# Routing the tokens of a mixture of experts inside the attention stage, and running 25 full tiles while the last batches are routed

## What is computed

```
x = x + xattn(layernorm(x), ctx, ctx, gates..., outnorm_weight)     # per head: C = (q k^T / sqrt(32)) * D; C / normalizer; C v; head norm
x = x + ffn(layernorm(x), w12, w3, gate_w)

scores = einsum('btd,ed->bte', x, gate_w)
topk_scores, topk_idx = top_k(scores, 2);  topk_probs = softmax(topk_scores)
h1, h2 = split(einsum('btd,ehd->bteh', x, w12));  hidden = silu(h1) * h2       # H = 512
y = sum over the row's two experts of prob * einsum('bteh,edh->bted', hidden, w3)
```

## Time and profile before

| | |
|---|---|
| median of 3 runs | 655.87 us (653.12 to 657.32) |
| profiled execution | 654.9 us, of it 653.1 us between first and last instruction |
| TensorE matmul / weight load | 564.8 us (86%) / 466.0 us (71%) |
| VectorE | 451.9 us (69%) |
| ScalarE | 348.5 us (53%) |
| POOL | 296.5 us (45%) |
| mean granted TensorE clock | 0.933 of full speed |

### The profile page before, as it was taken

The page is one execution under the profiler, slowest core; times in us unless marked ns, Lnnn a source line. Parts: engine busy times, 40 slices in busy tenths (PEclk is TensorE's granted clock), DMA queues, the critical chain, the costliest instruction groups (busy, mean ns, idle before and its releaser), DMA issues.

```text
span 653.1 us, 14222 instructions
## 1 busy us (share of the span) xinstructions
PE 564.8 (86%) x3612; PEld 466.0 (71%) x3613; DVE 451.9 (69%) x987; ACT 348.5 (53%) x769; POOL 296.5 (45%) x312
## 2 busy tenths in 40 slices
PE   3779879999989951239999999999999999999993
PEld 1334668888878840127888888888888888888882
DVE  4664586787777778946667677667767767767762
ACT  2456556777777755014555555555555555555551
POOL 5423136365455534032555555555555555555532
PEclk9899998999999955559999999999999999999998
DMA  7875336787776668921433333333333333433322
GB/s 231 252 225 162 91 93 185 200 212 197 210 219 172 193 161 244 279 50 17 66 50 50 62 51 50 62 52 50 62 52 50 59 54 49 59 55 49 59 40 24
DMA packets 66018, 73.44 MB, mean 112 GB/s; under 512 B 12762, under 2 KB 55776, under 8 KB 65984
## 3 DMA queue, kind: packets, MB, share of 16 engines
q0 software_dynamic: 18240, 28.17, 25.1%
q1 hardware_dynamic: 38528, 36.21, 19.1%
q10 hardware_dynamic: 9216, 8.65, 3.9%
HBM read 43.51 MB, written 19.01 MB: 96 GB/s over the span
## 4 chain that ended last, share of the span: by engine, by line
issue 40%; POOL 15%; PE 14%; DVE 14%; DMA 10%; ACT 4%; SPq 1%; ACTq 0%; DVEq 0%; POOLq 0%
POOL xg L1168 9%; DMA out_rows<-ys,index 6%; PE bank L1287 5%; POOL out_rows L1177 4%; PE dots L1269 3%; DVE ohn L996 2%; DMA w12h<-in_x 2%; DVE ohp L995 2%; DVE c L846 1%; DVE st L727 1%; PE dots L1222 1%; ACT x2n L636 1%; PE bank L1336 1%; PE dots L1220 1%; DVE tot L887 1%
## 5 line engine op out<-in xcount | busy, mean ns | idle before, releaser
L1177 POOL DMA_INDIRECT out_rows<-ys,index x71 | 112.5, 1585 | 156.1 <-DVE ys L1048 145.1
L1054 DVE TENSOR_TENSOR w3l<-w,w3h 128x1024 fp32r<-128x1024 f32 x71 | 87.2, 1229 | 30.9 <-issue 29.7
L1168 POOL DMA_INDIRECT xg<-token_table,index x71 | 70.4, 992 | 46.1 <-DVE index L1013 24.4
L693 ACT CAST w3h<-w 128x1024 fp32r x71 | 74.4, 1048 | 20.4 <-issue 20.4
L1409 PE MATMUL bank<-w3l,hth 128*128 128x256 f32 x284 | 76.5, 302 | 1.8 <-DVE w3l L1054 1.8
L1410 PE MATMUL bank<-w3h,hth 128*128 128x256 f32 x284 | 70.8, 282 | 0.0
L1287 PE MATMUL bank<-aug,c 128*128 128x99 f32 (+2 forms) x512 | 63.9, 279 | 6.0 <-DVE c L846 5.9
L1287 PEld LDWEIGHTS bank<-aug,c 128*128 128x128 f32 x512 | 60.8, 195 | 11.0 <-DVE c L846 10.3
L1048 DVE TENSOR_SCALAR ys<-bank,pc 128x256 f32<-128x256 f32 x71 | 34.4, 484 | 46.6 <-PE bank L1413 46.6
L1031 DVE TENSOR_TENSOR htl<-bank,hth 128x512 fp32r<-128x512 f32 x71 | 49.1, 692 | 25.2 <-ACT hth L683 25.2
L1381 PE MATMUL weighs<-w12l,xh 128*128 x144 | 62.3, 432 | 1.1 <-DVE xl L1020 1.1
(11 more groups left out here) (172 smaller groups left out, 1235.1 us busy)
## 6 DMA issues: line engine op xcount, KB each, us to landing
w12l<-in_w12T SPq DMA_DIRECT2D x24, 256.0 KB, 3.5
aug<-in_ctxv SPq DMA_DIRECT2D x16, 264.0 KB, 3.5
w12h<-in_x SPq DMA_DIRECT2D x16, 256.0 KB, 3.6
w12l<-in_ctxT SPq DMA_DIRECT2D x16, 256.0 KB, 3.6
qbd<-w12h SPq DMA_DIRECT2D x64, 64.0 KB
x<-in_x SPq DMA_DIRECT2D x16, 256.0 KB, 3.3
out_rows<-x ACTq DMA_DIRECT2D x16, 256.0 KB, 2.5
token_table<-x2n ACTq DMA_DIRECT2D x16, 256.0 KB, 3.5
```

The lines of the kernel that those rows point to most:

```text
L693: nc.scalar.copy(W3H[i][:], w3[:, bass.ds(e, 1)].rearrange("p a k d -> p (a k d)")).then_inc(w3h_ready, 1)
L1054: v.tensor_tensor(W3L[i][:], w3[:, bass.ds(e, 1)].rearrange("p a k d -> p (a k d)"), W3H[i][:].bitcast(F32), ALU.subtract).then_inc(w3l_re ...
L1168: q.indirect_dma_start(out=XG[x][:], out_offset=None, in_=table, in_offset=bass.IndirectOffsetOnAxis(ap=index[:, j:j + 1], axis=0)).then_i ...
L1177: q.indirect_dma_start(out=out, out_offset=bass.IndirectOffsetOnAxis(ap=index[:, j:j + 1], axis=0), in_=YS[o][:], in_offset=None, compute_ ...
```

## The change

Four parts, in this order through the kernel.

- *Routing in groups*: batches are routed in five groups, `GROUPS` (0 to 2, 3 to 5, 6 and 7, 8 to 11, 12 to 15). A row's rank within its expert is carried on from group to group (`seen`), its place is 4096 times the expert plus the rank, and POOL scatters pairs of row number and probability to these places of a table in memory (`place`, 64 scatters of 128 pairs of 8 bytes). A list of tiles is fetched from the table (`fetch_list`), turned by TensorE and copied into `index`, `prob`, `etab` and `clear`.
- *Two phases of tiles*: the first 25 (`FIRST`) tiles are full ones of batches 0 to 7 and are listed in step 15. Steps 16 to 18 and the separate routing are gone: what was in them stands in `remains(j)` of each engine, between the instructions of tiles 0 to 21. The first 28 tiles are written out, the others looped (VectorE writes out all).
- *Weight pieces*: the eight late ones are handled in steps 4 to 7, two in each (`load_free`, `free_pieces`, `free_low`); the low parts of the last two of the sixteen are made by VectorE (`last_low`). `piece_high` handles batch b-1 in step b, not b-2.
- *Third weights*: SyncE fetches the 512 KB of a tile's expert two tiles ahead (`load_w3`); `w3` is gone. The row's probability comes from `prob`, so `pc` and its wait are gone.

The diff's core, in the order of the engines' blocks: SyncE, ScalarE (`free_pieces`, `remains`), VectorE (the loop over steps), POOL.

```diff
+CUT = B // 2
+FIRST = (CUT * S * TOPK - NE * (P - 1) + P - 1) // P
+GROUPS = ((0, 3), (3, 6), (6, CUT), (CUT, 12), (12, B))
...
+            def load_free(s):
+                if s == 0:
+                    sp.wait_ge(cols_ready, 2)
...
+                for n in (2 * s, 2 * s + 1):
+                    at = (W1 + n) * HID
+                    sp.dma_start(room(flat_l, W1 + n, HID), w12T[:, at:at + HID]).then_inc(free_in, 16)
...
+            def load_w3(j, i):
+                wait(sp, w3l_ready, j - 1)
+                e = sp.value_load(etab[0:1, bass.ds(j, 1)], min_val=0, max_val=NE - 1)
+                sp.dma_start(W3[i][:], w3T[:, bass.ds(e * (KH * E), KH * E)]).then_inc(w3_in[i], 16)
...
+            def free_pieces(s):
+                act.wait_ge(free_in, 32 * (s + 1))
+                for n in (2 * s, 2 * s + 1):
+                    at = slice((W1 + n) * HID, (W1 + n + 1) * HID)
+                    nc.scalar.copy(flat_h[:, at], room(flat_l, W1 + n, HID)).then_inc(free_hi, 1)
+                act.wait_ge(free_hi, 2 * s + 1)
+                wait(act, free_added, 16 * s)
+                nc.scalar.mul(minus2[:], room(flat_h, W1 + 2 * s, HID), -1.0).then_inc(free_minus, 1)
...
+            def remains(j):
+                if j == 1:
+                    turned(B - 3)
+                    squares(B - 1, SQ[:])
+                if j == 2:
+                    row_scales(B - 2)
+                    head_scales(B - 1)
+                if j == 3:
+                    normal_rows(B - 2)
+                    store_rows(B - 2)
+                if j == 4:
+                    turned(B - 2)
+                if j == 5:
+                    row_scales(B - 1)
+                if j == 6:
+                    normal_rows(B - 1)
+                    store_rows(B - 1)
+                if j == 7:
+                    turned(B - 1)
+                if j == 9:
+                    odds(len(GROUPS) - 1)
...
+            for b in range(B):
+                i = b % 2
+                if has(b, 1):
+                    far(b - 1)
+                combine(b, 0)
...
+                    if b == hi + 3:
+                        largest(gr, 1)
+                        chosen(gr)
+                if has(b, 1):
+                    centre(b - 1)
...
+                    if b == hi + 4:
+                        slots(gr, RANKS)
+                        chances(gr)
+                        if gr == 2:
+                            counts(0, RANKS[:, 64:64 + NE])
+                if b == GROUPS[2][1] + 5:
+                    list_rows(0)
+                if has(b, 2):
+                    row_statistics(b - 2)
+                combine(b, 1)
+                if b == B - 1:
+                    take_list(0, RANKS)
...
+                    if b == hi + 2:
+                        largest(gr, 0)
+                if FREE_AT <= b < FREE_AT + FREE_STEPS:
+                    free_low(b - FREE_AT)
...
+            def place(g, lo, hi):
+                k0 = group(g)[2]
+                pool.wait_ge(slots_ready, g + 1)
+                pool.wait_ge(pairs_ready, g + 1)
+                for k in range(k0 + lo, k0 + hi):
+                    q.indirect_dma_start(out=places, out_offset=bass.IndirectOffsetOnAxis(ap=slot[:, k:k + 1], axis=0),
+                                         in_=pairs[:, k, :], in_offset=None).then_inc(placed, 16)
...
+                if has(b + 1, 0):
+                    weighted(b + 1, 1 - b % 2)
...
+                if b in (8, 9, 10):
+                    place(0, 4 * (b - 8), 4 * (b - 7))
+                if b in (11, 12):
+                    place(1, 6 * (b - 11), 6 * (b - 10))
+                if b == 13:
+                    place(2, 0, 5)
+                if b == 14:
+                    place(2, 5, 8)
...
             for j in range(NX - 1):
                 gather(j)
+            mix(B - 2)
             for j in range(TILES + 1):
...
+                if j == 3:
+                    mix(B - 1)
                 if j >= 1:
                     add(j - 1)
+                if j in (1, 2):
+                    place(3, 2 * (j - 1), 2 * j)
+                if 4 <= j < 10:
+                    place(3, 2 * (j - 2), 2 * (j - 1))
+                if 11 <= j < 19:
+                    place(4, 2 * (j - 11), 2 * (j - 10))
+                if j == 19:
+                    fetch_list(1)
```

More of the change, by code:

```diff
@@ L305, in expert_tiles, with has @@
                 step(TILES // NX * NX + x, x)
+        def has(b, back):
+            return 0 <= b - back < B
         def stages(j):
@@ new lines, in odds @@
+            def odds(g):
+                nt = group(g)[1]
+                act.wait_ge(r_diff, g + 1)
+                nc.scalar.activation(ex[:, 0:nt], diff[:, 0:nt], ACT.Exp).then_inc(r_exp, 1)
+            weights(0, 0)
+            for b in range(B):
+                i = b % 2
+                if has(b, 1):
+                    near(b - 1)
+                state(b, i)
+                if has(b, 3):
+                    turned(b - 3)
+                weights(b, 1)
+                if b == 0:
@@ L1056, in _ @@
+            last_low(B - 2)
+            take_scores(B - 4, SCORES)
+            last_low(B - 1)
+            far(B - 1)
             low(0, 0)
-            dve.wait_ge(w3_in, 16 * NE)
-            dve.wait_ge(tables, 1)
-            expert_tiles(dve, expert)
+            for j in range(TILES + 1):
+                expert(j, j % 2)
         @block.gpsimd
@@ L1384, in half_up @@
                     ins.then_inc(up_ready, 1)
+                if isinstance(j, int) and j == FIRST:
+                    pe.wait_ge(tables, 2)
                 if up:
```

1076 lines of the change are left out of this document (594 added, 482 removed).

## The result

The changed kernel takes 706.88 us, the kernel before 656.16 (medians of 4 runs each): ratio 1.073, 95% interval 1.061 to 1.085. Slower, as forecast, but by 51 us where 16 were forecast.

The account below looks back on a forecast made before the run. Bounds: mutual engine waits in attention, 61.8 us with nearly no matmul, then TensorE in the tiles. Terms: 654.9 - 56.9 + 14.8 + 3.6 + 16 + 28 + 7.8 + 3 = 671.2 us; range 628 to 692.

Parts of the forecast that it names:

- The gap: Between last attention matmul and first tile matmul: listing the first 25 tiles early lets tiles start at 233.3, gaining 56.9 us.
- Eight weight pieces: Steps 4 to 7: VectorE's tot waits behind ScalarE's casts, 3.7 us a step, +14.8 us; routing in steps 6 and 7, +3.6.
- 32 scatters: POOL, steps 8 to 14: 1.3 us each, half counting in the two-step loop, VectorE's 10.6 us beside: +16 us (11 to 26).
- The list in step 15: Seam after attention: list ready at 227.7, with 0.3 us for POOL to start, inside the gap's gain.
- Batches 13 to 15 inside the tiles: Early tiles: table loads and waits for statistics, +28 us; clock falls behind waits at tiles 2, 5 and 9, +7.8 us.
- POOL in tiles 11 to 18: POOL work of 5.5 us against 4.87 in eight tiles, partly covered by two ys buffers, plus expert turns: +3 us.
- Third weights: Tiles: 512 KB fetched per tile within 6.7 us of room, so hidden, cost 0.
- 1: Rival: inserted work fits into idle time, 618 us, chance 0.20; in one of two stages only, 642 to 647, 0.10.
- 2: Rival, cheap ends: placings at 0.58 us and no fall of the clock, 658 us, no difference; chance 0.20.
- 3: Rival: a placing costs what an adding scatter does, POOL becomes the bound in the tiles, 690 us; chance 0.10.
- 4: Rival: a table load costs the 2.83 us that the rows leave open, 686 us; chance 0.05.
- 5: Rival: third weights late in every tile, 7.5 us from issue to landing, 728 us; chance 0.03.

Follow-up runs that it names:

- b1: Kernel before, with nine more unused VectorE instructions (128x48) in each of steps 4 to 13, behind the first c: 678.71 us, +22.7.
- e3: Changed kernel with 20 filler matmuls of 128 columns in each of steps 5 to 8, ahead of the key-value product: 697.14 us.
- c5: c3 with e7's swap and ten filler matmuls in each of steps 6 to 15: 678.01 us, 2.9 more than without the filler.
- b2: Kernel before, with four more scatters of 128 pairs of 8 bytes behind vw in each of steps 4 to 13: 695.26 us, +39.3.
- c2: Changed kernel, placings ahead of vw, free weight pieces later in mid-step, mix ahead of step 15's list, one function table in tiles 2 and 5: 678.07 us.
- e1: Changed kernel with POOL's placings in steps 8 to 14 ahead of vw instead of behind it: 689.35 us, 14.8 less.
- c3: c2 with SyncE loading aug and kn ahead of the rows x: 672.98 us.
- e7: Changed kernel with SyncE's fetch of third weights two tiles ahead placed before the order of additions: 708.44 us, 4.3 more.
- e6: Changed kernel with third weights fetched for the first two tiles only, 69 of 71 fetches left out: 698.96 us, 5.2 less.
- e5: Changed kernel with one function table for logarithm and exponential in tiles 2 and 5, 6 loads for 10: 702.72 us, 1.4 less.
- after: Changed kernel as it is, second profiled execution, 703.67 us; that run's median 704.16 us, ratio 1.074.
- e4: Changed kernel with VectorE's routing moved from between the two c's to behind the second c and its row statistics: 711.25 us, 7 more.

## Why the prediction was right and wrong

*The gap: right.* Forecast -56.9 us; -55.9 from the last `c` to the first SiLU, 57.5 between the matmuls.

*Attention's clock, no term at all: the step that failed.* The forecast put a fall of the clock only behind "Waits of 4 us and more at tiles 2, 5 and 9", and priced the stalls in attention as if TensorE went on at full speed behind them. The stalls were not more than forecast: TensorE's idle time grew by 24.4 us in steps 4 to 14, where 34.4 were added up. Its busy time, forecast to stay, grew by 26.5 us there and by 27.6 over all of attention, at a granted clock of 0.81. Waits of 1.8 to 3.5 us brought the fall as well, in b1 waits of 1.9 to 2.0. How much of the 27.6 us a full clock would give back stays open: 3.4 to 8.5 us in steps 5 to 7 (e3), nothing in c5.

*Eight weight pieces, "+14.8", with "+3.6" of routing: right in mechanism, near in size by luck* (+20.3, and 21.5 to 25.8 in the five other profiles). VectorE waited for the casts as described, 3.84 us for 3.7. But TensorE's idle time grew by 12.1 us only, not 18.4, and 8.2 us of slower matmuls came on top.

*32 scatters, "+16": wrong, 30.6 us.* The price of 1.27 us was right. "In the two-step loop each costs half its price" was 0.65 us; in b2 a scatter costs 0.98, of which the stalls are some 0.47 and the slower matmuls as much. So the half price was high enough for the stalls and missed the clock behind them. "VectorE's 10.6 run beside that" failed too: the placings pushed the mix into VectorE's routing, five of whose instructions then took 12.3 us too long, and in four steps out of five TensorE's wait for `c` stood behind one of them. I followed POOL from `vw` to mix, but neither who waits for the mix nor who works beside it. That 32 times 0.98 is 31 us is no proof: with VectorE's instructions in these steps at b1's price the sum would be over 41. With the placings ahead of `vw` 9.8 us of these steps came back.

*The list in step 15, "0.3 for POOL to start": wrong by some 6 us.* `fetch_list` stands ahead of the mix and waits for the placings to land; VectorE's statistics then waited 4.38 us for the mix, ahead of the last `c`. That this order is the whole cause is not shown: c2, with the mix ahead of the list, has 2.5 us of TensorE's idle time there for 5.0, but still took 10.6 us, as e1 did without it (10.8); c3 took 7.8. The order alone was not run.

*Batches 13 to 15 inside the tiles, "+28", and their clock, "+7.8": right in mechanism, too high in sum.* Tiles 2, 5 and 9 took 6.9, 5.4 and 5.0 us more than 4.87 (forecast 5.7, 5.6 and 4.1, and 2.6 of clock each), tiles 3 and 6 3.1 each (2.3). Tiles 0 to 10 together lost 27.5 us of the 35.8, of which up to 4.7 were meant for all other tiles to 21.

*POOL in tiles 11 to 18, "+3": wrong.* Tiles 11 to 21 lost 14.0 us. Eight tiles at the 6.2 us of work that POOL has in each, for 4.87, are 10.6, so this is an estimate and the other 3.4 us are open; I had let two `ys` buffers cover most of it, but POOL never got its lead back.

*Third weights, "Hidden: 0": wrong by 5 to 9 us.* The fetch took 3.9 us from issue to landing in the median (6.2 in the chain above), within the room of 6.7, but it was issued late. I had measured the room from `w3l` and overlooked that SyncE's order, which waits for an addition to land, stands ahead of it. With that order changed (e7) nothing was won, since POOL was late as well. So e6, which leaves out the fetches and the waits for them together, does not say which of the two cost the 5 to 9 us. Why the additions take 2070 ns for the 1585 of the earlier trace rows stays open; it is not the fetches (e6).

*Rivals.* 1 (idle time holds the work) is out: 57 and 41 us in both stages. 2 is out: a placing takes 1.27 us and the clock falls. 3 came nearest in result, with POOL as the bound in tiles 11 to 18, but by another way: the price of a placing was 1.27 and not 1.9, and most of the rest was the clock. 4 is out (e5). 5 is out in its form: late in 13 tiles, not 71.

The range ended at 692 because each case raised one price; none raised what a stall costs.

## What to carry to other kernels

Where TensorE is nearly always busy, price an edit by what it delays, and then price the stall twice: as time, and as the slower matmuls behind it. Here stalls of 2 us were enough for that. Follow a delayed instruction to the next engine that waits for it, to what is queued behind that one, and to what it now runs beside. Before a redesign of a loop, look who waits longest in it: swapping two loads won 6 us, where the redesign lost 51.

## What the runs showed of the hardware

- VectorE instructions with inputs in SBUF were held up beside POOL's elementwise passes, for up to three passes of 1.2 to 1.3 us in a row: 3.17, 3.07 and 2.45 us for 0.2 above, five such in steps 8 to 14 of after. The Trainium skill (SBUF — State Buffer, Who interferes with whom) has VectorE with two SBUF inputs and POOL share a read interface, where the later one waits; the trace agrees, and shows that it may wait for several POOL instructions. L972 has one input from SBUF; the same section lets `tensor_scalar` take the shared ports in a two-port mode, and no run here shows whether it did. What this cost the total is open: e1 and e4 did not isolate it, and b1, where it was 0.7 us a step at most, had too little of POOL's passes beside its chains.
- The granted clock went to the lower of its levels (1.2 of 2.4 GHz) with each of the ten waits of 1.8 to 4.4 us that TensorE had in steps 5 to 15 of after, and not with the two of 1.04 us. In b1 five waits of 1.9 to 2.0 us each brought 6.8 us at that level; one of 1.88 us and one of 1.14 did not. With filler matmuls in the waits of steps 5 to 7 it stayed at 1.00 (e3).
- A table load is 1.28 us and nothing beside it: five in tile 2, each followed within 0.02 us.
